# Last batch of a fused attention kernel: an earlier spread of the maxima, half A's residual and norm moved forward, and the state-space inputs cut by token halves

## The chip, the cores and the metric

The kernel runs on one core of a Trainium2 chip. The metric is the device time of one execution in microseconds, as the median of several runs. A profiled execution gives the trace; its span is the time from its first to its last instruction.

## What is computed

The reference is a chain of six residual blocks on x of shape (8, 32, 256), here 256 tokens by 256 channels:

```python
x = x + L0_xattn(layernorm(x), ctx_2048, ...)  # self attention, and attention over 512 context rows a batch,
                                               # both rounded to fp8 and projected by wproj
x = x + L0_attn(layernorm(x), ...)             # state space block
x = x + L0_ffn(layernorm(x), ...)              # 8 experts, top 2
x = x + L1_xattn(layernorm(x), ctx_2048, mask)
x = x + L1_attn(layernorm(x), ...)
x = x + L1_ffn(layernorm(x), ...)              # weights looked up in a 16 entry table
```

The change is in the end of the first block and in the first part of the second:

```python
# end of block 1, for each of the 8 batches
p = softmax(scores)                 # 16 heads x 32 queries against 512 context rows
xout = p @ (ctx @ wv)
catq = fp8(clip(concat(core, xout) / proj_smooth))
x = x + catq @ wproj * scales
# block 2
n = layernorm(x)
x_conv = causal_depthwise_conv(n, conv_w, conv_b)     # 4 taps
Bmat, Cmat, delta = split(n @ Wxproj)
delta = softplus(delta)
h = scan(exp(A * delta), delta * Bmat * (x_conv @ Winproj))
x = x + (Cmat * h) @ Woutproj + D * x_conv
```

## The kernel before

Each engine has an order of instructions written out by hand, and semaphores tie the five orders together. A loop runs over the eight batches of the context (`step(b, k)`, k is the buffer of two). For each batch TensorE computes scores in four tiles of 128 context rows (`scores`), VectorE scales them and takes the maximum over tiles, TensorE turns the maxima (`maxima`, L442), VectorE reduces them, and TensorE spreads the result over all partitions by four transposes into bank 4 (`spread`, L449). VectorE subtracts it (`shift`, L809), ScalarE takes exponentials (`exponentials`, L614). One step later TensorE mixes the context rows by these weights in two halves of the channels (`mix(b, k, c)`, L459, banks 5 and 6) and sums the weights (`total`, L468, bank 2); ScalarE inverts the sum (`inverse`, L619 and L620); VectorE corrects the inverse and multiplies both banks by it (`normalise`, L815, L817, L822), which frees the banks. VectorE adds the weights up before the total (`sums`, L795, L796). Beside all this VectorE writes terms of the looked-up weights of block 6 (`term`, L667), which GpSimd adds up by DMA.

The last batch (7) is written out after the loop. The values of batches 6 and 7 are computed each by itself (`values_of`, L541), rounded to fp8 by six VectorE instructions (`quantize_heads`, L872 to L879), and projected (`project_out(j, ...)`, L494 and L495) for the two halves of the tokens: half A (j = 0) holds batches 0 to 3, half B (j = 1) batches 4 to 7. Half A's projection can run as soon as the rounding of batches 0 to 5 is done. A semaphore px_ready counts the products of `normalise`; `mix(7, 1, 0)` waits until it is 14. TensorE's order there is

```python
            step(7, 1, more=False)
            pe.wait_ge(sq_ready, 8 * B)
            project_out(0, range(NH), 4)
            mix(7, 1, 0)
            total(7)
```

After the last rounding comes the tail: residual (L903 for half A, L1429 for half B), norm by halves (`first_stats`, L1405 to L1408, and `first_normal`, L274 to L276 and L1413), a turn of each half by TensorE (`turn_half`, L1033), a copy into a padded buffer (`pad_half`, L1418), the matmuls of the state-space inputs (L1044) and VectorE's convolution of all tokens (L1443, L1448), whose result goes through a matmul (L1050). `keep_clock(n, nb)` issues n matmuls of 512 columns whose result nobody reads. ScalarE computes the softplus of delta from L1288 to L1290.

## Time and profile before

| what | us |
|---|---|
| median of 3 runs | 448.95 |
| lowest and highest run | 448.14, 449.51 |
| the profiled execution | 450.79 |
| its span | 449.0 |
| TensorE busy in it | 422.1 |
| VectorE busy in it | 361.1 |
| ScalarE busy in it | 254.9 |

The page gives busy time per engine over the whole span; a busy share says little about one stage. The rows further down are from the timeline of the stretch that the diff touches, from 301 to 339 us, and from windows behind it.

### The profile page before, as it was taken

The page shows a single profiled execution, that of the slowest core. Times are in us where ns is not written, and L with a number is a line of the kernel's source. Part 1 is how long each engine was busy: PE and PEld are TensorE (multiplying, and loading weights), DVE is VectorE, ACT ScalarE, POOL GpSimd, SP SyncE. Part 2 cuts the span into 40 slices and gives each one's busy share as a digit, 9 for nine tenths or more (in the row PEclk, how much of TensorE's full clock was granted, in tenths as well). Part 3 has the DMA queues.
Part 4 walks back from the last instruction along what each step waited for, and adds up shares of the span by engine and source line. Part 5 has one row for each costly group of instructions (what it writes and reads, how often), then busy time and mean ns, then how long its engine had stood idle before and what let it go on. Part 6 is the DMA issues. An engine that isn't in the chain of part 4 may idle for free.

```text
span 449.0 us, 6874 instructions
## 1 busy us (share of the span) xinstructions
PE 422.1 (94%) x2414; PEld 295.3 (66%) x2416; DVE 361.1 (80%) x758; ACT 254.9 (57%) x794; POOL 28.1 (6%) x39
## 2 busy tenths in 40 slices
PE   8999989999999999999999999998987999877797
PEld 3454345877885757677575875865663999636487
DVE  5889899898898687888999989877888897667531
ACT  3478878767647868748986677572113561221240
POOL 0010000210000001001000010100100201000000
PEclk9999999989999999999999999999999899999789
DMA  8498200501002026957328473891749879120000
GB/s 309 195 197 338 95 0 1 188 2 48 1 22 74 0 86 131 285 155 141 111 53 187 117 141 97 174 332 61 140 103 350 328 231 218 30 91 2 1 1 23
DMA packets 14047, 56.80 MB, mean 127 GB/s; under 512 B 1792, under 2 KB 2880, under 8 KB 12480
## 3 DMA queue, kind: packets, MB, share of 16 engines
q1 hardware_dynamic: 10560, 39.31, 23.8%
q0 software_dynamic: 3456, 17.11, 20.2%
q8 instruction: 17, 0.28, 0.2%
q14 instruction: 14, 0.11, 0.1%
HBM read 41.40 MB, written 0.26 MB: 93 GB/s over the span
## 4 chain that ended last, share of the span: by engine, by line
PE 73%; DVE 18%; ACT 5%; issue 2%; DMA 1%; DVEq 0%; ACTq 0%
PE PS L459 12%; PE PS L432 10%; PE PS L434 9%; PE PS L433 9%; PE PS L1764 4%; PE PS L1237 3%; PE PS L1110 3%; DVE small_dt.float L2064 2%; PE PS L509 2%; PE PS L1092 2%; PE PS L468 2%; PE PS L1095 1%; PE PS L1096 1%; PE PS L1097 1%; PE PS L541 1%
## 5 line engine op out<-in xcount | busy, mean ns | idle before, releaser
L583 ACT ACTIVATE sq_dt.float<-PS 128x128 bf16<-128x128 f32 x256 | 67.3, 279 | 32.8 <-PE PS L434 26.3
L459 PE MATMUL PS<-s_dt.float,ctx_ring_dt.float 128*128 128x512 f32 x128 | 57.7, 593 | 1.3 <-DVE px_dt.float L822 1.3
L432 PE MATMUL PS<-wkc_dt.float32r,ctx_hi_dt.float32r 128*128 128x512 f32 x128 | 54.1, 423 | 0.8 <-DVE ctxT_ring_dt.float32r L694 0.4
L583 ACT ACTIVATION_READ_ACCUMULATOR sq_dt.float<-PS 128x1 f32 x256 | 53.5, 209 | 0.0
L434 PE MATMUL PS<-wkc_dt.float32r,ctxT_ring_dt.float32r 128*128 128x512 f32 x128 | 51.0, 399 | 0.0
L433 PE MATMUL PS<-wkT_dt.float32r,ctx_hi_dt.float32r 128*128 128x512 f32 x128 | 50.7, 396 | 0.0
L1764 PE MATMUL PS<-wch_dt.float,xs_dt.float 128*128 128x512 f32 x96 | 42.0, 592 | 0.0
L459 PEld LDWEIGHTS PS<-s_dt.float,ctx_ring_dt.float 128*128 128x128 f32 x128 | 23.6, 190 | 25.0 <-issue 23.0
L660 ACT ACTIVATE luttmp_dt.float<-low_bit_dt.float,vec_dt.float,small_dt.float 128x1536 f32<-128x1536 uint8 x24 | 38.5, 1654 | 2.0 <-DMA lutw_dt.float<-luttmp_dt.float 2.0
L667 DVE SCALAR_TENSOR_TENSOR luttmp_dt.float<-idx_dt.float,luttmp_dt.float 128x1536 f32<-128x1536 uint8 x21 | 36.4, 1751 | 0.0
L432 PEld LDWEIGHTS PS<-wkc_dt.float32r,ctx_hi_dt.float32r 128*128 128x128 f32 x128 | 24.4, 191 | 13.1 <-ACT sq_dt.float L583 7.6
L673 POOL DMA_DIRECT2D lutw_dt.float<-luttmp_dt.float x21 | 17.9, 852 | 234.0 <-DVE luttmp_dt.float L667 234.0
L1764 PEld LDWEIGHTS PS<-wch_dt.float,xs_dt.float 128*128 128x128 f32 x96 | 17.9, 190 | 21.0 <-issue 20.6
L434 PEld LDWEIGHTS PS<-wkc_dt.float32r,ctxT_ring_dt.float32r 128*128 128x128 f32 x128 | 24.4, 190 | 5.7
L433 PEld LDWEIGHTS PS<-wkT_dt.float32r,ctx_hi_dt.float32r 128*128 128x128 f32 x128 | 24.6, 192 | 3.7
L432 PE MATMUL PS<-A_hi_dt.float32r,ctx_hi_dt.float32r 128*128 128x512 f32 x64 | 25.1, 392 | 0.6 <-DVE s_dt.float L709 0.6
L809 DVE TENSOR_TENSOR s_dt.float<-s_dt.float,PS 128x2048 f32<-128x2048 f32 x8 | 18.3, 2288 | 8.6 <-PE PS L449 8.6
L434 PE MATMUL PS<-A_hi_dt.float32r,ctxT_ring_dt.float32r 128*128 128x512 f32 x64 | 24.9, 390 | 0.0
L433 PE MATMUL PS<-A_dt.float32r,ctx_hi_dt.float32r 128*128 128x512 f32 (+1 forms) x64 | 24.9, 389 | 0.0
L709 DVE TENSOR_TENSOR s_dt.float<-PS,small_dt.float 128x512 f32<-128x512 f32 x32 | 21.5, 689 | 1.9 <-PE PS L434 1.1
L2064 DVE BATCH_NORM_STATS2 small_dt.float<-raw_dt.float 128x6 f32<-128x128 f32 x80 | 16.1, 278 | 1.4 <-ACT raw_dt.float L1877 1.3
L619 ACT ACTIVATE vecs_dt.float<-PS 128x512 f32<-128x512 f32 x8 | 4.8, 599 | 21.5 <-PE PS L468 21.5
(312 smaller groups left out, 877.5 us busy)
## 6 DMA issues: line engine op xcount, KB each, us to landing
lutw_dt.float<-luttmp_dt.float POOLq DMA_DIRECT2D x21, 768.0 KB, 6.5
wch_dt.float<-in_chunks SPq DMA_DIRECT2D x6, 1024.0 KB, 8.0
ctxT_ring_dt.float<-in_ctxT SPq DMA_DIRECT2D x8, 512.0 KB, 3.3
ctx_ring_dt.float<-in_ctx SPq DMA_DIRECT2D x8, 512.0 KB, 3.7
keysT_dt.float<-in_ctxT SPq DMA_DIRECT2D x8, 512.0 KB, 7.5
keys_dt.float<-in_ctx SPq DMA_DIRECT2D x8, 512.0 KB, 7.4
zu_dt.float<-in_wproj SPq DMA_DIRECT2D x1, 2048.0 KB, 7.4
A_first_dt.float<-in_wproj SPq DMA_DIRECT2D x1, 2048.0 KB, 7.9
```

The lines of the kernel that those rows point to most:

```text
L432: nc.tensor.matmul(o, x_hi, hi[:, c, :], start=c == 0, stop=False)
L433: nc.tensor.matmul(o, x_hi, lo[:, c, :], start=False, stop=False)
L434: last = nc.tensor.matmul(o, x_lo, hi[:, c, :], start=False, stop=c == CT - 1)
L459: last = nc.tensor.matmul(bank(5 + c), keysr[k][:, t, c * 128:c * 128 + 128], sS[k][:, t, :], start=t == 0, stop=t == KT - 1)
L583: last = nc.scalar.activation(sq[:, (4 * hf + g) * D:(4 * hf + g + 1) * D], bank(hf)[:, g * D:(g + 1) * D], ACT.Square, accum_out=ssq[:, k ...
L660: nc.scalar.activation(lutt[:, m, :], low_bit[:, m, :], ACT.Identity, scale=lut_gap[:, k:k + 1], bias=col("lut", 2 * k)).then_inc(lut_leaf, 1)
L667: nc.vector.scalar_tensor_tensor(lutt[:, m, :] if k else lutw[:, m, :], idx[:, m, :], float(2 * k), lutt[:, m, :], ALU.is_equal, ALU.mult) ...
L673: pool.dma_start(lutw[:, m, :], lutt[:, m, :], accum_op=ALU.add).then_inc(lut_added[m], 16)
L709: nc.vector.tensor_tensor(sS[k][:, t, :].rearrange("p (g q) -> p g q", g=G), score_bank(b, t, G, 64), krs[:, k, t, :].unsqueeze(2).broadca ...
L809: nc.vector.tensor_tensor(sS[k], sS[k], bank(4).unsqueeze(1).broadcast_to([128, KT, 512]), ALU.subtract)\
L1764: last = nc.tensor.matmul(bank(q), xs[:, VARIANT[n], c, j * 128:j * 128 + 128], wch[n % 2][:, c, hf * 512:hf * 512 + 512], start=c == 0, s ...
L2064: last = nc.vector.bn_stats(st[:, 8 * j + i, :], r[:, j, i * D:(i + 1) * D])
```

## The change

TensorE: in the step of batch 7 the spread is issued after two of the four tiles of the second mix of batch 6, and the rest of that mix and the total come behind it. The turn of half A stands ahead of half B's projection. The state-space inputs are computed for half A, then five `keep_clock` matmuls (eight before), the turn of half B, and the inputs for half B.

ScalarE: in that step `exponentials(7)` comes before `inverse(6)`.

VectorE: behind `shift(7)` the order is now a table term, `sums(7)`, `normalise(6)`, a table term. Residual and statistics of half A come next, its normalisation behind the first product of batch 7. The copy into the padded buffer and the convolution are done by token halves, half A's ahead of the residual of half B.

```diff
+        def turn_half(pe, k, j):          # moved out of the tail, with first_stats and first_normal
...
-                if prev:
+                if prev and more:
                     mix(b - 1, 1 - k, 1)
                     total(b - 1)
-                spread(b)
+                    spread(b)
+                elif prev:
+                    mix(b - 1, 1 - k, 1, range(2))
+                    spread(b)
+                    mix(b - 1, 1 - k, 1, range(2, KT))
+                    total(b - 1)
+                else:
+                    spread(b)
...
-            def mix(b, k, c):
+            def mix(b, k, c, tiles=range(KT)):
...
-                last.then_inc(pctx, 1)
+                if t == KT - 1:
+                    last.then_inc(pctx, 1)
...
+            turn_half(pe, 1, 0)
             project_out(1, range(8), 8)
             project_out(1, range(8, NH), 9)
...
-                if prev:
+                if prev and more:
                     inverse(b - 1)
...
                 exponentials(b, k)
+                if prev and not more:
+                    inverse(b - 1)
...
             shift(7, 1)
+            term(dve, LUT_STEPS, 0)
+            sums(7, 1)
             normalise(6, 0)
-            sums(7, 1)
             dve.wait_ge(core_added, 1)
...
-            term(dve, LUT_STEPS, 0)
             term(dve, LUT_STEPS, 1)
+            dve.wait_ge(proj_out, 1)
+            nc.vector.scalar_tensor_tensor(x[:, 0, :], bank(0)[:, 0:C], pscale, x[:, 0, :], ALU.mult, ALU.add)\
+                .then_inc(first_ready, 1)
+            dve.wait_ge(first_ready, 1)
+            first_stats(dve, self_step, 0)
             dve.wait_ge(r_ready, 8)
...
             nc.vector.tensor_tensor(px[:, 0, :, S:2 * S], bank(5, NH, S), R.rearrange("p (a q) -> p a q", a=NH),
                                     ALU.mult).then_inc(px_ready, 1)
+            first_normal(dve, self_step, 0)
             dve.wait_ge(v_full, 7)
             quantize_heads(6, 4, slice(0, NH))
...
                 quantize_heads(7, 7 if hf else 3, slice(8 * hf, 8 * hf + 8))
-                if hf == 0:
-                    dve.wait_ge(proj_out, 1)
-                    nc.vector.scalar_tensor_tensor(x[:, 0, :], bank(0)[:, 0:C], pscale, x[:, 0, :], ALU.mult,
-                                                   ALU.add).then_inc(first_ready, 1)
...
-            turn_half(1, 0)
-            keep_clock(8, 7)
-            turn_half(1, 1)
+            def ssm_inputs(j):
+                for i in (2, 0, 1):
+                    t0 = (i % 2) * T + 128 * j
+                    o = bank(2 + i // 2)[0:SSM, t0:t0 + 128]
+                    for c in range(CT):
+                        last = nc.tensor.matmul(o, w_ssm[:, c, i * SSM:(i + 1) * SSM], hpad[:, c, 4 * j:4 * j + 4, 3:S + 3],
+                                                start=c == 0, stop=c == CT - 1)
+                    if j == 1 and i != 0:
+                        last.then_inc(ssm_p, 1)
+
             pe.wait_ge(ld_w["ssm"], 48)
+            pe.wait_ge(half_padded, 1)
+            ssm_inputs(0)
+            keep_clock(5, 7)
+            turn_half(pe, 1, 1)
             pe.wait_ge(hT_ready, 1)
-            for i in (2, 0, 1):
-                o = bank(2 + i // 2)[0:SSM, (i % 2) * T:(i % 2) * T + T]
...
+            ssm_inputs(1)
...
+            def convolve(j):
+                b4 = slice(4 * j, 4 * j + 4)
+                for c in range(CT):
+                    last = nc.vector.tensor_scalar(xcv[:, c, b4], hpad[:, c, b4, 0:S], col("conv_w", 4 * c),
+                                                   col("conv_b", c), ALU.mult, ALU.add)
+                step(last)
+                for k in range(1, 4):
+                    for c in range(CT):
+                        last = nc.vector.scalar_tensor_tensor(xcv[:, c, b4], hpad[:, c, b4, k:S + k],
+                                                              col("conv_w", 4 * c + k), xcv[:, c, b4], ALU.mult, ALU.add)
+                    if k < 3:
+                        step(last)
+                return last
+
+            dve.wait_ge(hpad_zero, 1)
+            pad_half(0).then_inc(half_padded, 1)
+            dve.wait_ge(half_padded, 1)
+            step(convolve(0))
             dve.wait_ge(proj_out, 2)
             nc.vector.scalar_tensor_tensor(x[:, 1, :], bank(1)[:, 0:C], pscale, x[:, 1, :], ALU.mult, ALU.add)\
                 .then_inc(x_ready, 1)
...
-            pad_half(0)
-            first_normal(1)
+            first_normal(dve, step, 1)
             pad_half(1).then_inc(hT_ready, 1)
             dve.wait_ge(hT_ready, 1)
...
+            convolve(1).then_inc(conv_ready, 1)
```

## Rows read from the trace of the kernel before

**Rows 1.** The page: its first line, and part 1 (busy time of each engine).
```profile
span 449.0 us, 6874 instructions
...
PE 422.1 (94%) x2414; PEld 295.3 (66%) x2416; DVE 361.1 (80%) x758; ACT 254.9 (57%) x794; POOL 28.1 (6%) x39
```

**Rows 2.** Timeline, TensorE, 301 to 312 us: start, duration, line, count, idle before.
```profile
301.06 3.60 PE L459 MATMUL PS<-s_dt.float,ctx_ring_dt.float 128*128 128x512 f32 x8
304.49 1.02 PE L468 MATMUL PS<-vecs_dt.float,consts_dt.float 128*128 128x512 f32 x2
305.35 0.60 PE L449 MATMUL PS<-consts_dt.float,small_dt.float 128*128 128x128 f32 x4
...
311.07 3.67 PE L459 MATMUL PS<-s_dt.float,ctx_ring_dt.float 128*128 128x512 f32 x8 [1.30 <-DVE px_dt.float L822]
```

**Rows 3.** Timelines of VectorE and ScalarE, 305 to 323 us.
```profile
305.99 2.29 DVE L809 TENSOR_TENSOR s_dt.float<-s_dt.float,PS 128x2048 f32<-128x2048 f32 x1 [3.36 <-PE PS L449]
308.19 0.68 DVE L815 SCALAR_TENSOR_TENSOR vecs_dt.float<-PS,vecs_dt.float 128x512 f32<-128x512 f32 x1
...
309.64 1.29 DVE L822 TENSOR_TENSOR px_dt.float<-PS,vecs_dt.float 128x512 f32<-128x512 f32 x2
310.85 1.22 DVE L795 TENSOR_TENSOR vecs_dt.float<-s_dt.float 128x1024 f32<-128x1024 f32 x1
...
312.70 3.42 DVE L667 SCALAR_TENSOR_TENSOR luttmp_dt.float<-idx_dt.float,luttmp_dt.float 128x1536 f32<-128x1536 uint8 x2
316.93 0.69 DVE L885 SCALAR_TENSOR_TENSOR vecs_dt.float<-PS,vecs_dt.float 128x512 f32<-128x512 f32 x1 [0.81 <-ACT vecs_dt.float L620]
...
319.16 0.69 DVE L872 TENSOR_TENSOR qtmp_dt.float<-PS,small_dt.float 128x512 bf16<-128x512 f32 x1
...
321.33 0.69 DVE L879 TENSOR_TENSOR catx_dt.float32r<-qtmp_dt.float 128x512 fp32r<-128x512 bf16 x1
322.65 0.76 DVE L895 TENSOR_TENSOR px_dt.float<-PS,vecs_dt.float 128x256 f32<-128x256 f32 x2 [0.62 <-PE PS L459]
...
308.31 1.92 ACT L614 ACTIVATE s_dt.float<-s_dt.float 128x2048 f32<-128x2048 f32 x1 [1.50 <-DVE s_dt.float L809]
```

**Rows 4.** Timeline of all engines, 326 to 336 us.
```profile
327.23 0.48 DVE L903 SCALAR_TENSOR_TENSOR x_dt.float<-PS,small_dt.float,x_dt.float 128x256 f32<-128x256 f32 x1
...
327.62 0.41 DVE L872 TENSOR_TENSOR qtmp_dt.float<-PS,small_dt.float 128x256 bf16<-128x256 f32 x1
...
329.18 0.42 DVE L879 TENSOR_TENSOR catx_dt.float32r<-qtmp_dt.float 128x256 fp32r<-128x256 bf16 x1
...
331.56 0.28 PE L495 MATMUL PS<-A_first_dt.float32r,catx_dt.float32r 128*128 128x256 f32 x1
331.88 0.48 DVE L1429 SCALAR_TENSOR_TENSOR x_dt.float<-PS,small_dt.float,x_dt.float 128x256 f32<-128x256 f32 x1
...
335.17 0.43 DVE L1418 COPY hpad_dt.float<-PS 128x256 f32<-128x256 f32 x1 [0.53 <-PE PS L1033]
```

**Rows 5.** Timeline from 335 us; then two groups by shape (count, busy us, mean ns).
```profile
335.74 2.78 PE L1044 MATMUL PS<-hpad_dt.float,ssmw_dt.float 128*64 128x256 f32 x12 [0.61 <-DVE hpad_dt.float L1418]
336.40 2.71 DVE L1448 SCALAR_TENSOR_TENSOR moe_dt.float<-hpad_dt.float,vec_dt.float,moe_dt.float 128x256 f32<-128x256 f32 x6
...
337.74 0.51 ACT L1290 ACTIVATE moe_dt.float<-moe_dt.float,consts_dt.float 64x256 f32<-64x256 f32 x1
...
L1480 DVE TENSOR_TENSOR hT_lo_dt.float32r<-hT_dt.float,hT_hi_dt.float32r 128x256 fp32r<-128x256 f32 x2 | 0.8, 422 | 0.1
...
L1616 DVE TENSOR_TENSOR rotact_dt.float<-rotact_dt.float 128x128 f32<-128x128 f32 x2 | 0.6, 293 | 0.1
```

**Rows 6.** Windows: us, busy of each engine, granted clock, DMA share, GB/s.
```profile
345.00:349.00 4.00, 2.43 (x16) 1.47 (x14) 3.04 (x12) 1.25 (x4) 0.00 (x0) 0.98 1.05 393
349.00:353.00 4.00, 4.00 (x23) 4.00 (x23) 3.37 (x15) 0.15 (x1) 0.00 (x0) 0.59 1.01 399
...
424.00:432.00 8.00, 7.83 (x95) 7.37 (x96) 1.25 (x5) 3.72 (x7) 0.00 (x0) 0.58 0.01 2
```

More of the change, by code:

```diff
@@ L359, in score_bank @@
             return bank((2, 3, 2, 3)[t] if isinstance(b, int) and b == 0 else (2, 3, 7, 2)[t], *dims)
+        def turn_half(pe, k, j):
+            pe.wait_ge(ln_done, 2 * k + j)
+            for c in range(CT):
+                last = nc.tensor.transpose(bank(TURNED[k, j], CT, 128)[:, c, :], h[:, j, c * 128:c * 128 + 128], ident)
+            last.then_inc(turned, 1)
         busy = consts[:, 0:256].bitcast(bf16)
@@ L457, in mix @@
                         pe.wait_ge(px_ready, 2 * b)
-                for t in range(KT):
+                for t in tiles:
                     last = nc.tensor.matmul(bank(5 + c), keysr[k][:, t, c * 128:c * 128 + 128], sS[k][:, t, :],
                                             start=t == 0, stop=t == KT - 1)
-                last.then_inc(pctx, 1)
+                if t == KT - 1:
+                    last.then_inc(pctx, 1)
             def total(b):
@@ L1029, in tail_pe @@
         def tail_pe(pe):
-            def turn_half(k, j):
-                pe.wait_ge(ln_done, 2 * k + j)
-                for c in range(CT):
-                    last = nc.tensor.transpose(bank(TURNED[k, j], CT, 128)[:, c, :], h[:, j, c * 128:c * 128 + 128], ident)
-                last.then_inc(turned, 1)
-            turn_half(1, 0)
-            keep_clock(8, 7)
-            turn_half(1, 1)
+            def ssm_inputs(j):
[7 more added lines that the diff above has]
+                        last.then_inc(ssm_p, 1)
             pe.wait_ge(ld_w["ssm"], 48)
+            pe.wait_ge(half_padded, 1)
+            ssm_inputs(0)
+            keep_clock(5, 7)
+            turn_half(pe, 1, 1)
             pe.wait_ge(hT_ready, 1)
-            for i in (2, 0, 1):
-                o = bank(2 + i // 2)[0:SSM, (i % 2) * T:(i % 2) * T + T]
-                for c in range(CT):
-                    last = nc.tensor.matmul(o, w_ssm[:, c, i * SSM:(i + 1) * SSM], hpad[:, c, :, 3:S + 3],
-                                            start=c == 0, stop=c == CT - 1)
-                if i != 0:
-                    last.then_inc(ssm_p, 1)
+            ssm_inputs(1)
             pe.wait_ge(conv_ready, 1)
@@ L1424, in tail_dve @@
             nc.vector.memset(hpad[:, :, :, 0:3], 0.0).then_inc(hpad_zero, 1)
-            dve.wait_ge(first_ready, 1)
-            first_stats(0)
-            first_normal(0)
+            xcv = xc.rearrange("p c (b s) -> p c b s", b=B)
+            dt = bank(3)[0:SSM, 0:T]
+            def convolve(j):
[5 more added lines that the diff above has]
+                for k in range(1, 4):
+                    for c in range(CT):
+                        last = nc.vector.scalar_tensor_tensor(xcv[:, c, b4], hpad[:, c, b4, k:S + k],
[7 more added lines that the diff above has]
+            step(convolve(0))
             dve.wait_ge(proj_out, 2)
```

53 lines of the change are left out of this document (20 added, 33 removed).

## The prediction

> **What bounds the kernel now.** I read the page first: the span is 449.0 us and TensorE is busy for 94% of it [rows 1]. That share covers stages with different limits, so I went to the stretch that the diff touches, from the last batch's scores (297 us) to the start of the experts (349 us), and read its timeline engine by engine, then the chain of waits through it. The reader is to see four things.
>
> First, one real hole of VectorE and one of TensorE. VectorE has its maxima ready at 302.63 us (305.99 - 3.36) and then waits 3.36 us, because TensorE puts the second mix (3.4 us) and the total ahead of the four spreading transposes, which end at 305.95 [rows 2, 3]. TensorE has a hole of 1.30 us: the first mix of batch 7 starts at 311.07 and waits for VectorE's px product (L822), which ends at 310.93, while TensorE had been done with the output projection of half A since 309.77 [rows 2, 3].
>
> Second, from 311 us TensorE sets the pace (mix, total, values, mix: back to back), until VectorE's px product of batch 7 at 322.65 [rows 3].
>
> Third, from there the chain alternates: values matmuls, the rounding of one half of the heads, the residual of tokens A (L903 at 327.23), the rounding of the other half (ends 329.60), the last 16 projection matmuls (end 331.84), the residual of tokens B at 331.88 [rows 4]. The whole first norm of tokens A lies under those 16 matmuls and costs nothing today.
>
> Fourth, after that VectorE sets it: norm B, the padded copy, which ends at 335.60, and the convolution to 339.11 [rows 4, 5].
>
> **The change, part by part.** All times are those of the changed program on the clock of the profiled execution.
>
> *Spread inside the mix.* The spread moves ahead of half of the second mix (1.72 of 3.44 us) and of the total (0.86 us: 304.49 to 305.35). So the shift starts 2.58 us sooner, at 303.41; the maxima (302.63) are there before TensorE reaches the spread at 302.8. Instruction count and TensorE time do not change: the total then ends at 305.96 and half A's projection still ends near 310.
>
> *VectorE's new order behind the shift.* Before: shift, normalise(6), sums(7), two table terms. Now: shift, term, sums(7), normalise(6), term. The shift's start to the next start is 2.20 us [rows 3], so term 0 runs 305.61 to 307.32 (1.71, two took 3.42). The exponential, now ahead of the inverse on ScalarE, runs 305.73 to 307.65 (1.92). sums(7) then starts at 307.69 and takes 1.85 to the next start. normalise(6) takes 2.74 (308.19 to 310.93), so it ends at 307.69 + 1.85 + 2.74 = 312.28. The first mix of batch 7 needs both products of normalise(6) (px_ready 14), because it writes the banks that they read. It starts at 312.28 + 0.14 = 312.42 instead of 311.07: **+1.35 us**. The head start of 2.58 is spent on 1.71 (term) + 0.37 (waiting for the exponential) + 1.85 (sums). TensorE's hole grows from 1.30 to about 2.4 us. Total, values and second mix follow at +1.35: the inverse is there for VectorE at 318.28 (was 316.93), the second mix ends at 324.0.
>
> *Residual and norm of A moved forward.* Residual 0.48 and statistics about 0.8 us fall between term 1 (ends about 314) and the inverse at 318.28: VectorE waits there for 3 us anyway, so nothing. Behind them on its queue is only that same wait. The Newton steps and the normalisation (about 0.9 us) come after px[0], at 320.4; rounding of batch 6 starts at 321.3 rather than 320.5 and takes 2.86 (319.16 to 322.02 before), so it ends at 324.16, 0.1 behind the second mix. Without the idle 0.62 us that VectorE has there today [rows 3] it would cost 0.9. So px[1] starts at **+1.45**. ScalarE's two small steps for A come behind inverse(7), beside VectorE's own two steps on R. Then values, term 2 and the first rounding are all +1.45. The residual is gone from between the roundings: L872 starts 0.39 us after L903 [rows 4], so the second rounding ends at +1.45 - 0.39 = **+1.06**, 330.67.
>
> *The projection of B.* A turn of A (0.44 us) stands before it, inside the wait for the first rounding. Both halves run back to back and the second starts when the rounding is there, so its end is at 331.84 + 1.06 = 332.90. This is where the moved norm pays nothing: it used to lie under exactly these matmuls.
>
> *Convolution by token halves.* Its eight instructions become sixteen of half the length. The trace before has no such instruction; the nearest pair is a tensor_tensor of 128 columns at 0.293 us against 0.422 at 256 [rows 5]: 0.129 less, not half. Eight of them: 1.03 less than 3.51 us (335.60 to 339.11), 2.48 for each half, 4.96 for both. Lower bound 1.76 a half (strictly by size), upper 3.51 (no saving); I take 2.48, since that pair has the same two sizes on the same engine. The first half now stands between the last rounding and the residual of B: 330.75 + memset 0.1 + copy 0.43 + small gaps gives a start at 331.34 and an end at 333.82, while the projection is ready at 332.9. It overshoots by about **+0.88**: residual B starts at 333.82 rather than 331.88 (+1.94). What is queued behind it is the whole chain: statistics B, the turn, the padded copy. The second half is short by **-1.03**. So the convolution ends at +1.06 + 0.88 - 1.03 = **+0.91**, at 340.02. ScalarE's softplus does not bind: it ends at 338.25 before, 0.8 ahead of its reader [rows 5], and later inputs (+1.94) with a halved first matmul group leave it about 0.4 ahead.
>
> The Trainium skill ("Perfetto Trace Analysis", Optimizing Scalar/DVE Operations) says the same against this split: VectorE pays a data access of some 60 ns for each instruction, so larger operations are better where the engine is saturated; the same section recommends breaking instructions up where they hold up other engines. By its 60 ns the eight added instructions would cost an estimated 0.5 us, half a convolution about 2.0, and the sum would come out near 0 (449.0); the two rows above give 1.45 us for the split and stand.
>
> *ssm inputs by halves and keep_clock.* 24 matmul records of 128 columns in place of 12 of 256 (2.78 us, [rows 5]). The first twelve and five keep_clock matmuls fall in TensorE's wait for norm B (332.9 to about 336.5), the second twelve beside the second convolution; uncovered, each half would cost about 1.4. Three keep_clock matmuls less: nothing on the path, unless the clock falls (below). DMAs: none is added; the mask loads wait on loop_over and the keysT loads on proj_out, so both start about 1.06 later. Their readers come after the experts' first matmuls.
>
> **Sum.** +0.91 us. The profiled execution took 450.79 us (449.0 of it span); it would be 451.7. The median of the runs is 448.95, 1.84 lower, so I put the same difference on it: **449.9 us**, +0.2%. With the bounds of the half convolution: at 1.76 the overshoot is 0.16 and the gain 1.75, which would be -0.5, but softplus then binds at about -0.1: 448.85. At 3.51 it is 1.06 + 1.91 = +2.97: 451.9. About 0.3% (1.35 us) is what a measurement of this kernel tells from no change.
>
> **Rivals.**
>
> *Slower: the clock falls in the ssm stage.* Before, the granted clock is 0.98 of 2.4 GHz in 345 to 349 us and 0.59 in 349 to 353, after a stretch with TensorE busy 2.43 of 4.00 us [rows 6]. In the changed program TensorE is busy from 335.6 to 340.0 only for one turn and the second ssm inputs, some 2 of 4.4 us, against 2.78 us for the inputs alone before. If the clock goes to 1.2 GHz there, the price is at most that of the stretch in [rows 6]: a mean of 0.59 over 4 us is 3.3 us at half rate, in which TensorE does 1.6 us less. The ssm matmuls on the path, then keep_clock and the turns behind them would carry it. From +0.7 to +1.6: 450.6 to 451.5. It decides from 0.5 us on, where the time leaves the bound of no change. The Trainium skill ("TensorE: Matmul & The Clock Gate", HAM oscillation) warns that recurring waits of TensorE throttle its clock; the fall at 349 us agrees, and no run yet shows one at 340. Chance 0.22.
>
> *The change does what it says.* If the head start of the shift reached TensorE, the mix would start when the projection ends, at 310.0, -1.07 instead of +1.35, and the sum would be -1.5: 447.4. For it speaks only the wait row; against it the written order, which puts 3.6 us of VectorE work ahead of the product that the mix waits for. Chance 0.05.
>
> *Faster: a late low-clock stretch goes away.* In 424 to 432 TensorE is busy for 7.83 of 8.00 us at a mean of 0.58 [rows 6], so 6.7 of them are at half rate. A shifted tail could meet full clock for all of it or a part: at most 3.4 us less (446.5), for half of it 1.7 less (448.2). It decides from 2.3 us on. For it: nothing in the diff touches those stages. Chance 0.13, half of it below 447.6.
>
> *Same mechanism, convolution near its upper bound*: 451 to 451.9. Chance 0.10.
>
> **How the numbers follow.** The sum as worked out: 0.50, 448.8 to 450.9, a quarter of it above 450.3. Slower: 0.22 x 0.9 + 0.10 + 0.12 = 0.42. Faster: 0.04 + 0.07 + 0.01 = 0.12. Within 0.3%: 0.46. The range of 8 in 10 reaches from 447.9 to 452.0: on the fast side to the lower bound of the convolution with a little of the late clock, on the slow side over the upper bound of the convolution.
>
> **What would show it.** Right: the shift near 303.4; TensorE's wait before the mix of batch 7 at 2.4 us instead of 1.3; the residual of A near 314 in an idle of VectorE of about 3 us; the two roundings without a gap; the sixteen convolution instructions at 0.3 to 0.36 us, the first eight ending after the projection. Wrong: a mix that starts before 311.1; a convolution half under 2 us; a granted clock under 1.00 between 335 and 346, or 1.00 in 349 to 352.

## The result and the profile after

The changed kernel takes 453.24 us in the median of 9 runs (449.53 to 456.42), the kernel before 449.04 in 9 runs beside it (447.17 to 450.05). The ratio is 1.009, 95% interval 1.0059 to 1.012: slower by about 4 us. The forecast was 449.9 us with a range up to 452.0, and "within 0.3%" as its likeliest case. Ratios here and below leave out the few runs that lie over 1.5% above the fastest of their kernel, medians keep them, so the two need not divide exactly.

The page of the changed kernel, first line and busy times, against [rows 1]:

```profile
span 451.4 us, 6901 instructions
...
PE 421.9 (93%) x2423; PEld 293.3 (65%) x2425; DVE 363.2 (80%) x766; ACT 254.6 (56%) x794; POOL 27.2 (6%) x39
```

TensorE is busy as long as before, and at half rate for 17.1 us in all in either trace, in a span 2.4 us longer. So this trace has more idle time and no more half-rate time; what differs is where the half-rate stretches stand. The two spans are not a fair pair: the last step starts 1.56 us sooner in the changed trace, since in 90 to 100 us its granted clock is 1.00 where that of before is 0.83, in a stretch with no edit. VectorE's instructions stand within 0.05 us of each other in the two traces up to 90 us and 1.6 us apart from 137 us on. Measured from the start of the last shift, which frees the comparison from that and from the earlier spread, the stretch to the end of the span got 6.5 us longer; less the 2.57 us by which the shift moved ahead, the changed program loses 3.98 us. In what follows "+x" means this: the distance from the shift, changed minus before, minus 2.57.

TensorE's timeline at the mix of batch 7 in the changed kernel (start, duration, line, count, idle before):

```profile
310.88 3.67 PE L484 MATMUL PS<-s_dt.float,ctx_ring_dt.float 128*128 128x512 f32 x8 [2.67 <-DVE px_dt.float L851]
314.39 1.02 PE L494 MATMUL PS<-vecs_dt.float,consts_dt.float 128*128 128x512 f32 x2
```

And VectorE's, from the shift (L838) to the second product of batch 7 (L930):

```profile
301.86 2.29 DVE L838 TENSOR_TENSOR s_dt.float<-s_dt.float,PS 128x2048 f32<-128x2048 f32 x1 [0.79 <-PE PS L474]
304.06 1.75 DVE L696 SCALAR_TENSOR_TENSOR luttmp_dt.float<-idx_dt.float,luttmp_dt.float 128x1536 f32<-128x1536 uint8 x1
306.13 1.23 DVE L824 TENSOR_TENSOR vecs_dt.float<-s_dt.float 128x1024 f32<-128x1024 f32 x1 [0.32 <-ACT s_dt.float L643]
...
309.45 1.29 DVE L851 TENSOR_TENSOR px_dt.float<-PS,vecs_dt.float 128x512 f32<-128x512 f32 x2
...
312.32 0.48 DVE L914 SCALAR_TENSOR_TENSOR x_dt.float<-PS,small_dt.float,x_dt.float 128x256 f32<-128x256 f32 x1
...
316.81 0.69 DVE L919 SCALAR_TENSOR_TENSOR vecs_dt.float<-PS,vecs_dt.float 128x512 f32<-128x512 f32 x1 [3.15 <-ACT vecs_dt.float L649]
```

VectorE's wait for the spread shrank from 3.36 us [rows 3] to 0.79, as the edit meant it to. It spent all of that and more on the term and the sums that now stand ahead of the product (L851), and TensorE's hole grew from 1.30 [rows 2] to 2.67 us. The residual of half A (L914) stands in an idle stretch of VectorE, of which 3.15 us are left.

The tail of the changed kernel, all engines: the first convolution half (L1450, L1455), the projection's last matmul (L521), the residual of B (L1466), then the second halves and the first state-space matmuls that read the convolution (L1081):

```profile
329.97 0.60 DVE L1450 TENSOR_SCALAR moe_dt.float<-hpad_dt.float,vec_dt.float 128x128 f32<-128x128 f32 x2
...
330.61 1.92 DVE L1455 SCALAR_TENSOR_TENSOR moe_dt.float<-hpad_dt.float,vec_dt.float,moe_dt.float 128x128 f32<-128x128 f32 x6
...
331.24 0.28 PE L521 MATMUL PS<-A_first_dt.float32r,catx_dt.float32r 128*128 128x256 f32 x1
...
332.56 0.48 DVE L1466 SCALAR_TENSOR_TENSOR x_dt.float<-PS,small_dt.float,x_dt.float 128x256 f32<-128x256 f32 x1
...
336.42 2.52 PE L1067 MATMUL PS<-hpad_dt.float,ssmw_dt.float 128*64 128x128 f32 x12 [0.52 <-DVE hpad_dt.float L1437]
...
339.01 1.64 PE L1081 MATMUL PS<-moe_dt.float,ssmw_dt.float 128*64 128x256 f32 x4
```

Eight instructions of the half convolution take 2.56 us (329.97 to 332.53) where eight of double length took 3.51 [rows 4, 5]; the projection had ended at 331.52, so VectorE comes 1.04 us late to the residual. The windows that answer to [rows 6] (granted clock is the third number from the right):

```profile
333.00:337.00 4.00, 2.04 (x10) 1.09 (x11) 2.72 (x11) 0.79 (x4) 0.00 (x0) 0.97 0.33 96
337.00:341.00 4.00, 3.93 (x17) 2.71 (x16) 2.83 (x10) 2.99 (x6) 0.00 (x0) 0.60 0.90 304
353.00:357.00 4.00, 2.29 (x20) 2.09 (x18) 3.49 (x10) 3.71 (x6) 2.09 (x2) 1.00 0.86 290
357.00:361.00 4.00, 3.55 (x10) 2.92 (x11) 3.60 (x5) 2.31 (x2) 0.00 (x0) 0.57 0.66 256
```

The kernel before was at half rate at 349 to 352 us, at the start of the experts. The changed one is at half rate at 337 to 340, inside the state-space stage, then at full rate as the experts start, and at half rate again in 357 to 361, at the first expert's down matmuls. What stands ahead of that second fall is in the timelines of VectorE and GpSimd and the list of TensorE's waits:

```profile
354.10 1.01 DVE L1526 TENSOR_TENSOR small_dt.float<-small_dt.float 128x16 f32<-128x16 f32 x1
...
355.35 0.90 DVE L1528 TENSOR_TENSOR small_dt.float<-small_dt.float 128x16 f32<-128x16 f32 x1
...
361.04 0.88 DVE L1547 SCALAR_TENSOR_TENSOR x_dt.float<-PS,small_dt.float,x_dt.float 128x256 f32<-128x256 f32 x2 [0.40 <-PE PS L1141]
...
366.16 0.87 DVE L1547 SCALAR_TENSOR_TENSOR x_dt.float<-PS,small_dt.float,x_dt.float 128x256 f32<-128x256 f32 x2
```

```profile
354.04 1.04 POOL L1423 CAST mask_dt.float<-maskraw_dt.float 128x1024 f32<-128x1024 uint8 x1 [27.94 <-PE PS L1128]
355.18 1.05 POOL L1424 TENSOR_SCALAR mask_dt.float<-mask_dt.float 128x1024 f32<-128x1024 f32 x1
```

```profile
PE PS L1141 <- DVE moe_dt.float L1537: 2.2, 1, 2.2
```

Two router instructions of 16 elements take 1.01 and 0.90 us; the one between them, of the same shape, takes 0.17 and falls in GpSimd's gap. Each long one starts within 0.2 us of a GpSimd instruction of 1.04 or 1.05 us, which converts the mask of block 4, and ends with it. In the trace before the same two (L1503 and L1505) took 0.17 us each, and GpSimd's conversion came at 355.15, when they were done. It met another instruction there, VectorE's first of the second expert, which took 1.26 us where the one of the third expert took 0.42, and GpSimd's own second instruction took 1.89 us instead of 1.05:

```profile
355.15 1.16 POOL L1392 CAST mask_dt.float<-maskraw_dt.float 128x1024 f32<-128x1024 uint8 x1 [28.94 <-PE PS L1097]
356.42 1.89 POOL L1393 TENSOR_SCALAR mask_dt.float<-mask_dt.float 128x1024 f32<-128x1024 f32 x1
```

```profile
357.32 1.26 DVE L1510 TENSOR_SCALAR moe_dt.float<-moe_dt.float 128x512 f32<-128x512 f32 x1
```

So the kernel before has a meeting too, and the experiments below show that it cost nothing there. In the changed trace it falls on the chain that TensorE waits for. The product that the first down matmul waits for comes later by the meeting, and the first two sums of the experts (L1547) are 5.12 us apart (3.05 before). The eight matmuls behind that wait run at half rate:

```profile
357.45 3.55 PE L1141 MATMUL PS<-down_dt.float,moe_dt.float 128*128 128x256 f32 x8 [2.17 <-DVE moe_dt.float L1537]
```

Where the 3.98 us are, by landmarks of both traces:

| landmark | predicted | measured |
|---|---|---|
| mix of batch 7 starts | +1.35 | +1.37 |
| second product of batch 7 (L930) | +1.45 | +1.46 |
| second rounding ends | +1.06 | +1.25 |
| residual of B starts | +1.94 | +2.24 |
| convolution ends | +0.91 | +1.41 |
| output of the state-space block in x | +0.91 | +1.97 |
| first expert sum | +0.91 | +2.24 |
| second expert sum | +0.91 | +4.31 |
| end of the span | +0.91 | +3.98 |

### The profile page after: what moved, and what is told of

The parts are those of the page before. It is cut to its first block, busy times and chain, and to the rows that moved or that the text cites. A ratio compares the mean times of both kernels' runs of the same rounds, so it can differ in the third digit from the quotient of the medians.

```text
span 451.4 us, 6901 instructions
## 1 busy us (share of the span) xinstructions
PE 421.9 (93%) x2423; PEld 293.3 (65%) x2425; DVE 363.2 (80%) x766; ACT 254.6 (56%) x794; POOL 27.2 (6%) x39
## 4 chain that ended last, share of the span: by engine, by line
PE 69%; DVE 21%; ACT 5%; issue 3%; DMA 1%; SPq 0%; DVEq 0%; ACTq 0%
PE PS L484 11%; PE PS L457 10%; PE PS L459 9%; PE PS L458 9%; PE PS L1787 4%; PE PS L1141 3%; DVE small_dt.float L2087 2%; PE PS L1268 2%; PE PS L535 2%; PE PS L1123 2%; PE PS L1166 1%; PE PS L494 1%; DMA raw_dt.float<-in_wk_nat 1%; PE PS L1276 1%; PE PS L1802 1%
## 5 line engine op out<-in xcount | busy, mean ns | idle before, releaser
L838 DVE TENSOR_TENSOR s_dt.float<-s_dt.float,PS 128x2048 f32<-128x2048 f32 x8 | 18.3, 2289 | 6.1 <-PE PS L474 6.1
L1141 PE MATMUL PS<-down_dt.float,moe_dt.float 128*128 128x256 f32 x64 | 16.8, 410 | 2.2 <-DVE moe_dt.float L1537 2.2
L643 ACT ACTIVATE s_dt.float<-s_dt.float 128x2048 f32<-128x2048 f32 x8 | 15.2, 1903 | 5.5 <-DVE s_dt.float L838 5.5
```

The costliest lines, as they stand in the source:

```text
L838: nc.vector.tensor_tensor(sS[k], sS[k], bank(4).unsqueeze(1).broadcast_to([128, KT, 512]), ALU.subtract)\
L1141: last = nc.tensor.matmul(o[:, j, :], am[k][:, m, j * 128:j * 128 + 128], wdn[:, e, m * C:(m + 1) * C], start=m == 0, stop=m == CT - 1)
```

## The experiments

Each kernel was timed beside the kernel before on the same chip, so each has a ratio of its own to it. Theory A: the written order and the halved tail lengthen the chain, as summed, and nothing else counts. Theory B: most of the loss is what a later or fuller TensorE sets off, the clock and the meeting of GpSimd with VectorE. Medians of 12 runs (9 for the changed kernel, 6 for its repetition):

| kernel | median us | ratio | 95% |
|---|---|---|---|
| changed | 453.24 | 1.0090 | 1.0059 to 1.0120 |
| changed, repeated | 454.59 | 1.0102 | 1.0046 to 1.0158 |
| front only | 452.09 | 1.0063 | 1.0033 to 1.0093 |
| tail only | 450.85 | 1.0011 | 0.9976 to 1.0046 |
| changed, normalise first | 447.94 | 0.9975 | 0.9938 to 1.0012 |
| changed, more keep_clock | 452.98 | 1.0076 | 1.0039 to 1.0113 |
| changed, hole filled | 451.86 | 1.0071 | 1.0034 to 1.0108 |
| changed, mask later | 451.07 | 1.0027 | 0.9990 to 1.0063 |
| changed, hole filled and mask later | 451.41 | 1.0033 | 0.9997 to 1.0069 |
| normalise first, taps spread | 446.65 | 0.9955 | 0.9916 to 0.9995 |
| the same, mask later | 447.34 | 0.9954 | 0.9924 to 0.9984 |
| before, mask later | 448.77 | 0.9988 | 0.9954 to 1.0022 |
| before, full rate into the experts | 449.92 | 1.0015 | 0.9985 to 1.0046 |

### Front only: the kernel before with the new order of the last step, and the old tail

```diff
+                elif prev:
+                    mix(b - 1, 1 - k, 1, range(2))
+                    spread(b)
+                    mix(b - 1, 1 - k, 1, range(2, KT))
+                    total(b - 1)
...
             shift(7, 1)
+            term(dve, LUT_STEPS, 0)
+            sums(7, 1)
             normalise(6, 0)
-            sums(7, 1)
```

> The kernel before with the front of the change alone: spread inside the mix, VectorE's order shift, term, sums, normalise, term, and the exponential ahead of the inverse. Theory A (the front costs what its order says): the mix of batch 7 starts 1.37 us later against the start of the last step, and all of it reaches the end, about +1.4 us over before (ratio 1.003). Theory B (the granted clock in the tail carries the loss): the tail is that of before, so +1.4 only if the clock behind it falls as before; without the ssm stage's clock fall the ratio stays under 1.004. Theory C (the early spread pays): -1 us.

Slower by 0.63% (2.8 us). TensorE's wait ahead of the mix is again 2.67 us, and the second product comes at +1.37. The tail is untouched and still the experts' sums are 5.64 us apart, with a 2.2 us wait ahead of the first down matmul. In this trace the front alone both costs its 1.4 us and has the later loss, and in time it costs more than 1.4 us, if only just: the lower bound is 0.33%, 1.5 us. All three theories on record had put it lower. The clock does not fall in the state-space stage here (1.00 in 333 to 341 us).

### Tail only: the changed kernel with the front taken back

```diff
-                elif prev:
-                    mix(b - 1, 1 - k, 1, range(2))
-                    spread(b)
...
             shift(7, 1)
-            term(dve, LUT_STEPS, 0)
-            sums(7, 1)
             normalise(6, 0)
+            sums(7, 1)
+            term(dve, LUT_STEPS, 0)
```

> The changed kernel with the front taken back (spread behind the total, inverse before the exponential, normalise before sums and terms); the moved residual and norm of A and the halved convolution and inputs stay. Theory A (the front is the loss): the ratio to before is 1.000 or a little under, since the first rounding follows as before and the rest is +0.6 us. Theory B (the halved tail starves TensorE and its clock falls at about 337 us and again in the experts): +2 to +3 us, ratio 1.005 to 1.007, with a granted clock near 0.6 in the 4 us before the state-space output, as in the changed kernel.

The ratio 1.0011 can't be told from no change. Its VectorE timeline shows a cost of the moved residual that the changed kernel hides:

```profile
314.11 0.48 DVE L905 SCALAR_TENSOR_TENSOR x_dt.float<-PS,small_dt.float,x_dt.float 128x256 f32<-128x256 f32 x1
...
315.30 0.15 DVE L296 TENSOR_SCALAR small_dt.float<-small_dt.float 128x1 f32<-128x1 f32 x1
315.49 0.69 DVE L910 SCALAR_TENSOR_TENSOR vecs_dt.float<-PS,vecs_dt.float 128x512 f32<-128x512 f32 x1
```

Behind the old front, residual and statistics (1.34 us) reach past the moment when the inverse is ready: the wait of 0.81 us [rows 3] is gone, and the correction L910 starts 0.5 us later after the shift. Its first expert sum comes 0.44 us later than before: the tail costs about half a microsecond. A half-rate stretch of 6.8 us in this profile (347 to 354) then makes the second one 1.88 us late; the timed ratio, with a bound of 0.46% or 2.1 us, doesn't settle how often that happens. Its clock is at 1.00 in 333 to 341 us too: of the two parts of the change neither alone brought the fall in the state-space stage, which stands in both profiles of the changed kernel and in the two with the hole filled.

### Normalise first: the changed kernel with the inverse and the product ahead of the sums

```diff
             term(dve, LUT_STEPS, 0)
-            sums(7, 1)
             normalise(6, 0)
+            sums(7, 1)
...
-                if prev and more:
+                if prev:
                     inverse(b - 1)
...
-                if prev and not more:
-                    inverse(b - 1)
```

> The changed kernel with VectorE's order behind the shift put as shift, term, normalise(6), sums(7), term, and the inverse ahead of the exponential. Theory A (the order is the front's whole loss): TensorE's wait before the mix of batch 7 goes from 2.67 us to under 0.5, the mix starts 2.3 us sooner, and the time is 2.3 us under the changed kernel (ratio to before about 1.004 where the changed kernel has 1.009). Theory B (the clock behind it): the same mix start, but the end differs by anything from 0 to -4 us, with the half-rate stretches in other places.

Two calls swapped on VectorE and the inverse put back ahead of the exponential on ScalarE, and 0.9975 instead of 1.009: the intervals do not touch. The two swaps were not run apart, and 0.9975 itself can't be told from no change. TensorE's timeline at the mix:

```profile
308.66 3.67 PE L484 MATMUL PS<-s_dt.float,ctx_ring_dt.float 128*128 128x512 f32 x8 [0.40 <-DVE px_dt.float L849]
```

The hole is 0.40 us, the product starts 5.33 us after the shift instead of 7.59, 2.26 sooner. The difference of the ratios is 1.15%, 5.2 us, so more than the chain went away with it. In its trace the clock is at half rate from 347.3 to 354.1, as the experts start, the mask conversion comes at 355.83 when VectorE's last instruction of 16 elements (353.21) is over, and that one takes 0.17 us: the meeting is not on the router's chain. This profile has another half-rate stretch of 6.8 us from 323 to 330, and its run (450.13 us) is slower than the median, so it does not show where the 5.2 us went.

### More keep_clock in the state-space stage

```diff
-            keep_clock(5, 7)
+            keep_clock(10, 7)
             turn_half(pe, 1, 1)
+            keep_clock(2, 7)
...
             ssm_inputs(1)
+            keep_clock(3, 7)
```

> The changed kernel with ten keep_clock matmuls in place of five ahead of the turn of half B, two behind the turn and three behind the inputs of half B: 10 more of about 0.21 us, all in TensorE's idle time. Theory A (VectorE's sums alone): no change to the changed kernel, within 0.3 us. Theory B (the clock): granted clock 1.00 through 333 to 345 us, the four matmul records L1081 at 1.08 us in place of 1.64, so at least 0.6 us less, and 2 to 3 us less if the later fall in the experts goes with it.

Windows of this kernel, and the matmul that took 1.64 us in the changed one:

```profile
333.00:337.00 4.00, 3.68 (x20) 1.85 (x20) 2.72 (x11) 0.82 (x5) 0.00 (x0) 1.00 0.41 126
337.00:341.00 4.00, 3.67 (x22) 2.15 (x20) 3.33 (x11) 3.15 (x6) 0.00 (x0) 1.00 0.84 283
...
357.00:361.00 4.00, 4.00 (x15) 3.28 (x15) 3.46 (x6) 1.53 (x1) 0.00 (x0) 0.60 0.52 196
```

```profile
338.81 1.08 PE L1083 MATMUL PS<-moe_dt.float,ssmw_dt.float 128*64 128x256 f32 x4 [0.31 <-DVE moe_dt.float L1457]
```

The clock holds through the stage and the state-space output comes at +1.41 instead of +1.97. So the fall there costs 0.56 us up to that output (0.46 at the second expert sum), and that is its whole price. The clock falls at the down matmuls all the same, and the ratio 1.0076 can't be told from 1.009. The rival of the prediction (the clock in the state-space stage) did happen, and it is the small part of the loss.

### The changed kernel again

> The changed kernel as it is, for a second profile and for times beside the next three. Theory A (the loss is the order and the halved tail, 1.4 + 0.6 us, and the rest is where the half-rate stretches happen to fall): the ratio comes out near 1.005 and this profile's half-rate stretches stand elsewhere. Theory B (the changed order brings about a later loss): 1.008 or more, with the loss of 2 us between the first two expert sums (3.05 us before, 5.12 us in the changed kernel's profile) there again.

1.0102, and the same places: mix at +1.37, L1526 and L1528 1.01 and 0.90 us, 2.2 us ahead of the first down matmul, 5.11 us between the expert sums. The chain behind the shift repeats to a few hundredths.

### The hole filled with matmuls that nobody reads

```diff
             project_out(0, range(NH), 4)
+            pe.wait_ge(shifted, 8)
+            keep_clock(9, 4)
             mix(7, 1, 0)
```

> The changed kernel with nine keep_clock matmuls (about 1.9 us at full rate) in TensorE's hole of 2.67 us before the mix of batch 7. Theory A: no change (within 0.3 us in the trace), the mix starts at the same place after the shift (9.0 us). Theory B (in some executions the hole lets the clock fall, and the mixes behind it run at half rate): 1 to 2 us less on average and less half-rate time per run.

The wait is 0.70 us and the mix starts no later. 1.0071 against 1.009 and 1.0102: a smaller number, with intervals that overlap. The run alone doesn't prove that the hole costs more than its length.

### The mask conversion later on GpSimd

```diff
             pool.wait_ge(proj_out, 2)
-            pool.wait_ge(gu_full, 3)
+            pool.wait_ge(gu_full, 5)
             step(nc.gpsimd.tensor_copy(mask, mask_u8))
```

> The changed kernel with GpSimd's conversion of the mask held back until the third expert's gate matmuls. Theory A (when the experts begin at full rate, GpSimd's conversion runs together with VectorE's router chain and stretches two of its small instructions from 0.18 to 1.01 and 0.90 us): both back at 0.18 us where the experts start at full rate, TensorE's wait of 2.2 us before the first down matmuls goes to about 0.7 us, and 1 to 2 us less on average. Theory B (the long small instructions come from something else): they stay at 0.9 to 1.0 us and the time does not change.

1.0027, from 1.009 and 1.0102: the ratio is 0.6 to 0.75% lower for one wait constant on an engine that is 6% busy. The intervals overlap, and the medians (451.07 against 449.33) are 0.39% apart, so this run alone does not prove it. Its profile does not test theory A either: the two instructions take 0.18 and 0.17 us, but the clock is at half rate from 350.8 to 357.7, as the experts start, and four other profiles with such a start and the mask in its old place (before, tail only, normalise first, taps spread) have them at 0.17 or 0.18 us as well. The profile with both edits, further down, is the test.

The profile caught the hole at half rate instead. TensorE's timeline and the windows over it:

```profile
310.53 6.69 PE L484 MATMUL PS<-s_dt.float,ctx_ring_dt.float 128*128 128x512 f32 x8 [2.66 <-DVE px_dt.float L851]
```

```profile
309.00:313.00 4.00, 2.47 (x3) 1.18 (x4) 3.90 (x7) 0.00 (x0) 0.66 (x1) 0.60 0.50 98
313.00:317.00 4.00, 4.00 (x6) 1.54 (x5) 0.27 (x2) 0.00 (x0) 0.19 (x1) 0.55 0.86 172
```

With the same wait ahead of it the mix takes 6.69 us, not 3.67: 3.0 us more, in front of everything that follows. Of five profiles with a hole of 2.67 us (changed twice, front only, more keep_clock, this one) one shows it. That is a loss that one profile of a kernel is likely to miss. Taken at one in five it would be 0.6 us in the mean, which is an estimate from very few profiles.

### Both: the hole filled and the mask later

> The changed kernel with both edits: nine keep_clock matmuls in the hole before the mix of batch 7, and the mask's conversion later. Theory A (order and halved tail cost the 1.97 us that the trace shows up to the state-space output, the hole's clock and the mask's collision the rest): ratio 1.0010 to 1.0050, at or under that of the later mask alone (1.0027), and no half-rate stretch between 305 and 335 us. Theory B (something else in the changed kernel costs the rest): 1.006 or more.

1.0033, with an interval that reaches theory B at its upper end (1.0069). This profile starts the experts at full rate. The two router instructions, the wait and the window of this kernel:

```profile
355.75 0.17 DVE L1528 TENSOR_TENSOR small_dt.float<-small_dt.float 128x16 f32<-128x16 f32 x1
...
356.17 0.17 DVE L1530 TENSOR_TENSOR small_dt.float<-small_dt.float 128x16 f32<-128x16 f32 x1
```

```profile
PE PS L1143 <- DVE moe_dt.float L1539: 1.4, 1, 1.4
```

```profile
357.00:361.00 4.00, 2.64 (x16) 2.46 (x17) 3.87 (x6) 3.96 (x5) 0.00 (x0) 1.00 0.96 368
```

```profile
358.36 1.96 PE L1143 MATMUL PS<-down_dt.float,moe_dt.float 128*128 128x256 f32 x8 [1.41 <-DVE moe_dt.float L1539]
```

Its only difference to the kernel with the filled hole is the mask. The wait ahead of the down matmul is 1.4 us instead of 2.2 (the expectation of the run before had said 0.7), the clock stays at 1.00 there, the eight down matmuls take 1.96 us and not 3.55, and the second expert sum comes 61.99 us after the shift instead of 64.27: 2.28 us in two traces that agree to 0.05 us up to the state-space output. What is left, 0.33% or 1.5 us, is near the +1.97 us that the trace shows up to that output. Beside 1.0027 for the mask alone, filling the hole gained nothing that these runs can tell. In time, the four kernels with the changed order and the mask in its old place have 1.0071 to 1.0102, these two with the mask later 1.0027 and 1.0033. No pair is clear of noise, but the weighted means are 0.5% apart, 0.2 to 0.85% (an estimate that takes the intervals as independent): 2.4 us, like the 2.28 us of the traces.

### The kernel before with the mask later, and with full rate into the experts

```diff
-            pool.wait_ge(gu_full, 3)
+            pool.wait_ge(gu_full, 5)
```

> The kernel before with GpSimd's conversion of the mask held back until the third expert's gate matmuls. Theory A (the collision hits the kernel before too, but only in executions where the experts begin at full rate): 0 to 1.5 us less than before, ratio 0.997 to 1.000, less than the 2.9 us that the same edit brought to the changed kernel. Theory B (the edit is worth the same anywhere): about -2.9 us, ratio 0.9935.

```diff
-            keep_clock(11, 6)
+            keep_clock(15, 6)
             turn_half(2, 0)
             turn_half(2, 1)
+            keep_clock(3, 0)
```

> The kernel before with seven more keep_clock matmuls around the turns ahead of the router (four before the turns, three behind), all in TensorE's idle time, so that the experts begin at full rate. Theory A (a full rate start exposes the router chain to the mask's conversion and leaves TensorE idle behind the first gate matmuls): granted clock 1.00 through 346 to 353 us, two small instructions of VectorE at 0.9 to 1.0 us, a wait of about 2 us before the first down matmuls, and 1 to 2.5 us slower than before (ratio 1.002 to 1.0055). Theory B (more clock is more speed): 1 to 1.6 us faster.

The second tests theory B with none of the change in it. VectorE and GpSimd, and a window:

```profile
353.54 1.00 DVE L1504 TENSOR_TENSOR small_dt.float<-small_dt.float 128x16 f32<-128x16 f32 x1
...
354.78 0.90 DVE L1506 TENSOR_TENSOR small_dt.float<-small_dt.float 128x16 f32<-128x16 f32 x1
```

```profile
353.47 1.04 POOL L1393 CAST mask_dt.float<-maskraw_dt.float 128x1024 f32<-128x1024 uint8 x1 [27.41 <-PE PS L1098]
```

```profile
357.00:361.00 4.00, 4.00 (x28) 3.79 (x29) 3.88 (x7) 2.35 (x3) 0.00 (x0) 1.00 0.53 204
```

```profile
356.88 1.97 PE L1111 MATMUL PS<-down_dt.float,moe_dt.float 128*128 128x256 f32 x8 [2.16 <-DVE moe_dt.float L1515]
```

The meeting with the router's chain appears in the old kernel once TensorE enters the experts at full rate. With the mask in its old place, all six profiles with a full-rate start have it and all four with a half-rate start have not. Both kernels ran that stage at full rate in their profiles. Counted from the shift, the second expert sum lands 0.74 us later than before with the meeting (h4) and 0.01 us sooner without it (mask later): the meeting by itself costs 0.75 us, the 2.2 against 1.4 us of TensorE's wait. The profile of the mask later also shows that the half-rate stretch at 349 us in the trace before cost nothing there, nor did the meeting of that trace with the second expert. And since its edit acts only behind the start of the experts, the kernel before can enter them at full rate by itself: the meeting is no property of the change, only its weight in the mean may be. In time 1.0015 and 0.9988 are both no change. So the collision is reproduced, its price in time here is not: the clock did not fall behind it in this trace, and that fall is what costs most in the changed one (eight down matmuls in 3.55 us, here in 1.97 behind the same wait).

### Taps spread over the waits, and the same with the mask later

On top of "normalise first", the first half of the convolution is cut at its taps: two ahead of the residual of B, one behind its statistics, one behind its normalisation.

```diff
-            step(convolve(0))
+            step(taps(0, 0))
+            step(taps(0, 1))
             dve.wait_ge(proj_out, 2)
...
             first_stats(dve, step, 1)
+            step(taps(0, 2))
             dve.wait_ge(loop_over, 3)
             first_normal(dve, step, 1)
+            step(taps(0, 3))
```

> The kernel with shift, term, normalise, sums (inverse ahead of the exponential), and of the halved convolution of half A only the first two taps ahead of half B's residual; tap 2 goes into VectorE's wait for ScalarE, tap 3 into its wait for the turn. Theory A (the overshoot of the first half convolution past the projection, 1.0 us in the changed kernel, is what the halved tail costs): half B's residual starts within 0.1 us of the projection's end, the tail saves 0.8 us against the run with normalise first, so 0.8 to 2 us under the kernel before (ratio 0.9955 to 0.998). Theory B (the halved convolution costs in its total length, 1.6 us): no gain over the run with normalise first.

> The best version so far with the mask's conversion held back. Theory A: 0 to 2 us under the best version, ratio to before 0.991 to 0.9955. Theory B (nothing is left of the collision there): the same 0.9955 as without it.

0.9955 and 0.9954, both faster than the kernel before. VectorE's timeline of the first:

```profile
329.86 0.48 DVE L1462 SCALAR_TENSOR_TENSOR x_dt.float<-PS,small_dt.float,x_dt.float 128x256 f32<-128x256 f32 x1 [0.41 <-PE PS L521]
...
331.25 0.61 DVE L1452 SCALAR_TENSOR_TENSOR moe_dt.float<-hpad_dt.float,vec_dt.float,moe_dt.float 128x128 f32<-128x128 f32 x2
331.90 0.16 DVE L274 TENSOR_TENSOR small_dt.float<-small_dt.float 128x1 f32<-128x1 f32 x1
```

The residual of B waits 0.41 us for the projection again, where the changed kernel came 1.04 us late, and the third tap fills the 0.51 us for which VectorE waited for ScalarE. Here the mask's place makes no difference: the first profile starts the experts at half rate, without a meeting on the router's chain.

## Why the prediction was wrong

**What held.** The front went as summed: spread 2.57 us sooner (2.58), the head start spent on term and sums, TensorE's hole 2.67 us (2.4), the mix at +1.37 (+1.35), the residual of A free in a wait of VectorE, the second product at +1.46 (+1.45). Normalise first shows that the order behind the shift, on VectorE and ScalarE together, is the cause of that term: with it put back, the hole is 0.40 us.

**What was mis-sized.** Taking the residual from between the roundings saved 0.21 us, not 0.39: the next rounding starts 0.53 us after the start of the last instruction of the one before, where it was 0.74. The half convolution took 2.56 us (2.48) and the overshoot was 1.04 (0.88). From the residual of B to the end of the convolution the second half saved 0.83 us, not 1.03. Together the convolution ends at +1.41, not +0.91. The Trainium skill ("Perfetto Trace Analysis", Optimizing Scalar/DVE Operations) gives about 60 ns of data access for a VectorE instruction on SBUF. Here two halves take 5.12 us for 3.51, which is 0.20 us for each of the eight added. The measurement decides; the price from the row of the same size was close.

**What failed.** The step "**Sum.** +0.91 us", which takes the end of the convolution for the end of the effect and carries it through the experts as a plain shift. 2.6 of the 4.0 us arise behind it:
- +0.56 in the state-space matmuls, from the clock that fell at 337 us. This was the slower rival, priced at 0.7 to 1.6. With ten more keep_clock matmuls it is gone and the output comes at +1.41.
- +2.34 between the state-space output and the second expert sum. No part of the prediction looked at GpSimd there. The mask conversion waits on gu_full, which the experts' first matmuls drive. With those at half rate, as in [rows 6], it falls behind the router's small instructions; with them at full rate it falls on them. That costs 0.75 us by itself (the kernel before at full rate, in its trace). The rest, 1.6 us, is the eight down matmuls at half rate: 3.55 us for 1.96. The profile with both edits has neither; that the fall follows from the longer wait is argued. The window 349 to 353 at 1.00 stood in the prediction as a sign of something wrong, but with no price.
- -0.3 from there to the end. Both traces have late half-rate stretches, before at 417 to 431 and after at 395 to 402 and 422 to 426. They nearly cancel, so the faster rival played no part.

The prediction also priced TensorE's hole at its length alone and set its clock rival only in the state-space stage. One profile shows 3.0 us for a hole whose clock fell. How much of the median this is stays open: filling it gave 1.0071 against 1.009 and 1.0102, and nothing with the mask later. The profile before was itself one with a costly half-rate stretch: that at 96 to 100 us, worth 1.6 us, is missing in 11 of the 14 profiles, and it is most of the 1.84 us by which the profiled execution lay above the median.

A rule of the Trainium skill would have pointed at the second of these: "SBUF — State Buffer" (SBUF: two separate sides) says that VectorE and GpSimd share a port pair under an exclusive lock; a VectorE instruction with two SBUF inputs meets a GpSimd one that reads SBUF, and whoever starts first blocks the other for its whole instruction. The rows agree: 16 elements in 1.01 and 0.90 us beside 1.04 and 1.05 us of GpSimd, 0.17 between them.

What stays argued and not shown: why the clock falls behind the 2.2 us wait in the changed kernel, its repetition, front only, more keep_clock and hole filled, but not in the kernel before at full rate with the same wait. Nor do the runs show how often each kernel enters the experts at full rate, or what makes it so; so the split of the 4 us by landmarks is that of one pair of traces (repeated to 0.05 us at every landmark by the second profile of the changed kernel), and its weight in the median is not measured.

## What to carry to other kernels

When work is moved ahead into a wait, place what the bounding engine waits for first; here the order of a few calls decides between 0.9% slower and no slower (0.9975, at most 1.0012). A sum that ends where the edit ends is incomplete if the next stage starts at another clock: list what on each engine, an idle GpSimd too, is released by that stage's progress, and ask what it will meet. Judge a tuned kernel by timed runs, since one profile can miss a half-rate stretch of 3 us or show one that costs nothing.

## What the runs showed of the hardware

- A GpSimd conversion of 128x1024 (1.04 us) holds back a VectorE instruction of 128x16 until it is done: 1.01 us instead of 0.17. It did so in six profiles, with the old order and the new, at the same two instructions. In the trace before, a tensor_scalar of 128x512 took 1.26 us beside it instead of 0.42, and the GpSimd instruction 1.89 us instead of 1.05.
- A half-rate stretch of 3.4 us can cost nothing (the start of the experts in the kernel before), 0.56 us (state-space matmuls), 1.6 us (first down matmuls), or, when it is twice as long, 3.0 us (a mix of 8 matmuls of 512 columns, 6.69 for 3.67). At the start of the experts one of 6.8 us cost 1.4 us, in three profiles (tail only, normalise first, mask later), where 3.4 us cost nothing.
- The granted clock of an untouched stretch differs between profiles (0.83 and 1.00 in 90 to 100 us), also between the two profiles of the changed kernel, whose last shifts start at 301.86 and 303.43 us. It moves a span by about 1.6 us, more than the effect that was forecast.
